# A branch hint at the head of every loop turn, on every engine

## The reference

```python
# 1: window attention with fake quantization (fq: int8 rounding by a scale from the tensor's largest value)
xw = windows of 7x7 pixels                       # 1024 windows, 49 tokens, 192 channels
q, k, v = split(fq(xw) @ fq(Wqkv).T + bqkv);  q, k, v = fq(q*SCALE), fq(k), fq(v)
attn = fq(einsum('bhmc,bhnc->bhmn', q, k)) + fq(bias)      # 12 heads of 16
attn = softmax(fq(attn));  out = fq(attn @ v) @ fq(Wout).T + bout
# 2: ConvNeXt block
y = depthwise_conv_7x7(x) + dw_b;  y = layernorm_channels(y) * ln_g + ln_b
y = gelu(y @ w1 + b1);  y = global_response_norm(y);  return x + y @ w2 + b2
```

## Time and profile before

| | us |
|---|---|
| three timed runs: median (lowest to highest) | 5646.66 (5645.17 to 5656.78) |
| the profiled execution | 5641.34 |
| its span, from the first to the last instruction | 5639.0 |
| qkv_range, qkv, range stages (rounded windows) | 270, 425, 650 |
| attention, project, conv, MLP loops (rounded windows) | 1275, 380, 460, 1090 |

### The profile page before, as it was taken

One profiled execution on the slowest core, in us unless ns is written; L12 is line 12 of the kernel. 1 busy time (PEld: TensorE's weight loads), 2 busy tenths in 40 slices (PEclk: granted clock), 3 DMA queues, 4 the chain that ended last, 5 costly groups with the idle time before them and its releaser, 6 DMA issues. The chain is left out here.

```text
span 5639.0 us, 117675 instructions
## 1 busy us (share of the span) xinstructions
PE 4267.6 (76%) x40394; PEld 2607.0 (46%) x40394; DVE 4318.8 (77%) x7490; ACT 3015.7 (53%) x5346; POOL 1539.3 (27%) x1649
## 2 busy tenths in 40 slices
PE   0787995555548777777774566699759999999999
PEld 0334553222226666666664444344334555555454
DVE  6898996999999888888886555000079999999986
ACT  0764672000008777777773556344355666666664
POOL 1103331000006555555554322000022222222220
PEclk9996555555559999999997777899969999999999
DMA  7864664333333332332332677788711222222222
GB/s 298 218 171 128 197 193 115 64 65 63 66 55 80 80 82 75 81 82 75 80 82 69 247 286 245 270 289 286 254 57 60 93 85 86 83 81 83 78 72 66
DMA packets 226218, 724.24 MB, mean 128 GB/s; under 512 B 34954, under 2 KB 132746, under 8 KB 205194
## 3 DMA queue, kind: packets, MB, share of 16 engines
q1 hardware_dynamic: 182346, 524.67, 32.4%
q0 software_dynamic: 43584, 195.21, 10.1%
HBM read 428.25 MB, written 291.50 MB: 128 GB/s over the span
## 5 line engine op out<-in xcount | busy, mean ns | idle before, releaser
L866 ACT ACTIVATE attn_int<-p_psum,scalars 128x588 int8<-128x588 f32 x512 | 384.8, 752 | 1045.6 <-PE p_psum L534 1020.9
L789 POOL TENSOR_TENSOR exp_lo<-exp,exp_hi 128x294 f16<-128x294 f32 x1024 | 779.6, 785 | 559.5 <-ACT exp_hi L860 556.6
L1551 PE MATMUL out_psum<-gelu_hi,w_parts 128*128 128x448 f16 x2016 | 605.3, 355 | 58.0 <-DVE w_parts L1727 30.9
L534 PE MATMUL range_psum<-q_diag,k_diag 128*128 128x196 bf16 x1536 | 364.8, 373 | 330.8 <-DVE p_min L652 328.7
L885 DVE SCALAR_TENSOR_TENSOR logit_int<-attn_int,scalars,bias_products 128x588 f16<-128x588 int8 x512 | 502.7, 982 | 124.7 <-ACT attn_int L866 96.4
L1623 DVE BATCH_NORM_STATS2 ln_stats<-z_img 128x6 f32<-128x192 f32 x448 | 125.9, 343 | 557.4 <-DMA z_img<-zd 556.9
L1587 ACT ACTIVATE gelu_pair<-h_psum,b_rows,w_unscale 128x448 f32<-128x448 f32 x448 | 324.8, 729 | 412.8 <-PE h_psum L1503 248.8
L831 PE MATMUL o_psum<-a_v,exp_hi 128*128 128x34 f16 x6144 | 383.1, 179 | 209.7 <-DVE a_o L909 191.5
L1287 PE MATMUL conv_psum<-c_in,toeplitz 128*128 128x448 f16 (+1 forms) x2304 | 469.7, 366 | 60.8 <-DMA dwb<-in_L_conv_dw_b_dram 60.6
L1503 PE MATMUL h_psum<-ln_parts_T,w_hi 128*128 128x448 f16 x2016 | 493.8, 354 | 18.8 <-DVE w_in L1686 16.9
L1551 PE MATMUL out_psum<-gelu_lo,w_parts 128*128 128x448 f16 x1344 | 475.7, 354 | 0.0
(11 more groups left out here) (313 smaller groups left out, 10008.2 us busy)
## 6 DMA issues: line engine op xcount, KB each, us to landing
k_diag<-kd SPq DMA_DIRECT2D x128, 384.0 KB, 5.1
toeplitz<-gd SPq DMA_DIRECT2D x48, 1024.0 KB, 16.5
yd<-y_out POOLq DMA_DIRECT2D x16, 2880.0 KB, 26.9
c_in<-yd SPq DMA_DIRECT2D x24, 1920.0 KB, 9.2
zd<-c_out POOLq DMA_DIRECT2D x24, 1792.0 KB, 13.7
z_img<-zd SPq DMA_DIRECT2D x16, 2688.0 KB, 9.2
x_chunk<-in_x_dram SPq DMA_DIRECT2D x12, 3136.0 KB, 9.9
x_img<-in_x_dram SPq DMA_DIRECT2D x16, 2352.0 KB, 16.0
```

What stands on the lines that cost most here:

```text
L534: last = nc.tensor.matmul(out[:, g, 0:HG * N], kt[:, g].rearrange("p o n -> p (o n)")[:, j::UP], q[:, g, :, j * N:(j + 1) * N], start=True ...
L789: last = nc.gpsimd.tensor_tensor(el[r][:, :, 2 * a, 0:N], src[:, :, a], eh[r][:, :, 2 * a, 0:N], ALU.subtract)
L866: nc.scalar.activation(a1[l % 2][:].rearrange("p (g n) -> p g n", g=G), pp[:, 0:G, 0:HG * N], ACT.Copy, scale=col(s, CP)).then_inc(a1d, 1)
L1551: last = nc.tensor.matmul(po[:, t, 0:TCH], w, hx[:, f, cols], start=f == 0 and x == 0, stop=f == NF - 1 and x == len(steps) - 1)
```

## The change

A new function `loop` opens a loop on one engine with a branch hint, and `peeled`, `images` and `turns` use it in place of `eng.Fori`. The first instruction of each turn, on each engine, then names the compare-and-branch at the end of the turn and says that it is likely taken. The rest of the program is as it was; the loop's bodies are one instruction longer, and all code behind a loop lies one instruction further on for each loop ahead of it on its engine. A loop that runs at most once would get no hint; there is none here.

```diff
+def loop(eng, first, end):
+
+    return eng.bass.Fori(first, end, engines=[eng.engine], hint_back_edge=True)
+
 def peeled(eng, n, body):
     body(0, True)
     if n > 1:
-        with eng.Fori(1, n) as i:
+        with loop(eng, 1, n) as i:
             body(i, False)
...
         def images(eng, image):
             image(0, True, lambda k: True)
-            with eng.Fori(1, IMG // 2 - 1) as i:
+            with loop(eng, 1, IMG // 2 - 1) as i:
                 image(i, False, lambda k: True)
...
         def turns(eng, turn):
             turn(0, True, True, True, True)
-            with eng.Fori(1, IMG - 3) as i:
+            with loop(eng, 1, IMG - 3) as i:
                 turn(i, False, True, True, True)
```

## The result

The changed kernel takes 5679.06 us (median; the runs lie between 5661.9 and 5717.9), the kernel before beside it 5645.91 us. The ratio is 1.0063, with an interval from 1.0048 to 1.0078. So the change makes the kernel slower, by about 0.6%, where I had forecast 5590 us. Its profiled execution has a span of 5677.7 us against 5639.0 us before, 38.7 us more.

A forecast was written before the change was run, and what follows sets the result against it. The prediction took TensorE's 14 attention back-edges, stalled on instruction fetch, as the bound. 5641.3 - 59 saved + 2 for hints = 5584 us, forecast as 5590 us since the timed median lies 5.3 us higher; range 5570 to 5655 us.

The forecast's parts named there:

- What bounds the kernel: Attention loop: TensorE's taken back-edge, median 5.29 us, 14 times, waits for instruction fetch and holds all engines.
- Taken away: TensorE's 14 attention back-edges go from 5.29 to 0.215 us, 5.08 us each, 71 us, all on the path.
- late next: Block behind TensorE's attention loop head: 127 instructions last 3.3 us, so up to 1.8 us of waiting returns each turn.
- the case that it works: Likeliest case, attention branch finds its target in place: 59 us saved, 5590 us (5571 to 5606), chance 0.45.
- A prefetcher that looks one block ahead has 6.6 us of warning: TensorE's attention branch: argument against the hint coming too late; 256 instructions at 26 ns give some 6.6 us.
- The head moves on by 3: TensorE's attention loop head shifts by three earlier loops' hints, leaving about 127 instructions in its block instead of 130.
- Comes too late: Rival: TensorE's attention hint gives only 0.2 us of warning or is ignored; 5641 to 5647 us, chance 0.32.
- Served second: Rival: at TensorE's attention branch the useless next block is fetched before the target; 62 us slower, 5709 us, chance 0.15.
- moves on a block: Rival: attention branch finds its target, but the block behind the head's waits; about 20 us saved, 5627 us, chance 0.08.
- The hints' own cost: One hint per turn and engine, 86 turns, about 0.05 us each: 4 us uncovered, taken as 2 us.
- Slower: Whole kernel slower than before: chance 0.15, from the target being fetched second at TensorE's attention branch, 5709 us.
- wrong altogether: Sign: another engine's small loop begins to fetch every turn, with q14 packets inside loops; no size given.

The follow-up runs named there:

- Slot 100: Kernel before with TensorE's attention loop head at instruction 100 of its fetch block: 5630.8 us without hint (0.9983), 5560.3 us with that loop's hint (0.9866).
- slot 157: Kernel before, no hints, TensorE's attention loop head put at instruction 157 of its fetch block, as in the changed kernel: 5656.9 us, 1.0041.
- slots 148: Kernel before with TensorE's attention loop head at instruction 148 of its fetch block: 5658.3 us without hint (1.0025), 5666.3 us with it (1.0035).
- slot 40: Kernel before plus TensorE's attention hint alone, loop head at instruction 40 of its fetch block, branch at instruction 175 of its own: 5575.9 us, 0.9886.
- slot 0: Kernel before plus TensorE's attention hint alone, loop head at the first instruction of a fetch block, branch at instruction 135: 5640.2 us, 0.9991.

## Why the prediction failed, step by step

**What bounds the kernel: right.** The 14 back-edges of TensorE in attention are on the path. Slot 100 shows it: with the branch at 0.45 us, VectorE's 5 us gap is gone and the time falls by 70.5 us.

**"Taken away": right in size, wrong in whether.** I had 71 us for all 14. Between slot 100 without and with the hint the branches shrink by 14 x 4.83 = 68 us, and the kernel by 70.5 us. A hinted branch costs 0.45 us, not the 0.215 us that I took. In the changed kernel the term is zero.

That 68 and 70.5 us nearly agree is partly luck, for two terms cancel. A mean turn is 5.20 us shorter in the traces. Of that, 4.83 us is the branch, and another 1.2 us is won from the branch to the first edge: without the hint TensorE's clock falls to the lower level at each of the 14 branches, with it the clock stays at the upper one at ten of them (58 us at the lower level over the loop instead of 143). The first edge then takes 1.3 us back. This last is what I had as "late next" (1.8 us). The clock was in my sum nowhere. With the head well placed the whole change saves 71 us, more than the 59 that I took for the case that it works.

**"A prefetcher that looks one block ahead has 6.6 us of warning": the step that failed.** From it I gave the likeliest case its 0.45, and the sum its -59 us; what came of that term is 0. The trace of before already spoke against it: 13 packets for 13 blocks, none behind the branch's own. The step from there to "nothing is fetched between the entry to the block and the branch, so nothing can be redirected" was written down as a rival and not believed. The hint worked with the branch 4.7 us behind the entry to its block (slot 175), failed in 12 of 14 turns at 3.0 us (slot 135), and here it had 0.4 us.

The Trainium skill (Runtime: NRT & Kernel Launch, section "Instruction fetch mechanics") says that prefetch is purely sequential. The traces of the kernel before and of the changed one agree with that. Slot 100 contradicts it: 12 packets instead of 13 a turn and a back-edge of 0.45 us say that a hint can turn one fetch away from the sequence. The measurement decides.

**"The head moves on by 3": wrong, and the source of the loss.** It moved by 31. I counted the instructions that TensorE itself gains and took that for the shift. The changed kernel then has 99 instructions behind its head instead of 127, and the next block is late by 1.0 to 1.9 us in every turn. I had expected that penalty (1.8 us) only as the price of a cured branch. It came behind uncured branches: 130 instructions had been enough cover for the next block, and 99 are not. My sum held no term for it, nor for VectorE's 4.9 us at the start of the stage, which probably has the same root.

**"Comes too late": the right rival with the wrong time.** Its mechanism is what happened, and TensorE's one hint alone gives its time (5649.1 us beside 5646.3 us; I had 5641 to 5647 us). For the whole change it lacked the term of the moved code: the place of TensorE's loop alone costs 0.41%, 0.22 to 0.60%, and hints on the other engines, which move the code nearly as far, 0.44%. The changed kernel's 0.63% (0.48 to 0.78%) lies at the upper end of both. VectorE's halt, which the place alone does not have, is 4.9 us or 0.09% of it. Whether anything is left beyond that can't be told within these intervals.

**"Served second" and "moves on a block": did not occur.** The branch never took 8 to 10 us as a rule (longest 6.4 us in the changed kernel), and by the packet counts the redirected fetch replaces the useless one instead of standing behind it. Two single branches look like the former, in kernels without a hint on this loop: 7.23 us (slot 157) and 7.69 us (hints on the other engines), each with two packets 0.3 and 0.5 us apart and 14 in the turn.

**The hints' own cost: within what I took.** Medians of 31 to 41 ns each (56 ns at most) against my 50 ns, and nothing measurable with all of them beside slot 100. What the runs show of their cost comes through where they push code.

**The chances.** Slower had 0.15, all of it from one mechanism that did not occur. My sign for "wrong altogether", packets of q14 inside the loops, did not show either (44 in the whole run, 43 before). What happened, a shift of code against fetch blocks on TensorE itself, stood in my text as a fixed number instead of as an unknown with two ends. A head anywhere in its block would have been the honest bound, and slots 100 to 157 without a hint span 0.9983 to 1.0041. The median came out 24 us above the top of the range.

## What to carry to other kernels

A branch hint pays only for a loop whose body does not stay on the engine, and only if the branch lies far enough behind the first instruction of its own fetch block: here it worked at 175 instructions or more and failed at 135 (12 of 14 turns) and at 36 or fewer. Put the loop's head so that both hold, the branch late in its block and plenty of code left behind the head, and leave the loops whose branches take 0.2 us alone. Any edit, even one to another engine's program, can move a large loop against its fetch blocks by enough to cost 0.4%, so before a small loss is explained by what an edit does, see whether the halts have moved. And price an idle stretch of TensorE with the clock behind it, not by its own length alone.

## What the runs showed of the hardware beyond that

- A branch hint takes a median of 31 ns on ScalarE, GpSimd and SyncE (41 ns on SyncE in the MLP), 39 ns on VectorE and 31 to 40 ns on TensorE.
- With its target in time, a hinted back-edge of the large loop takes 0.37 to 0.48 us at slot 100; those of TensorE's small loops take 0.21 us without a hint and 0.22 us with one.
- A taken branch to a block that is not there costs about the same whatever its place: medians of 5.2 to 5.5 us in all kernels where it is cold.
- Entering a placed loop costs one taken branch more, 0.19 us where its block has come (slots 148 and 157) and 5.2 to 5.5 us where not (slots 0 to 100); with every hint and slot 100 it was 0.56 us.
- The entry to the branch's block and the next packet lie 1.6 us apart at slot 100 and 3.0 us at slot 40; at slot 0 mostly no packet comes within the 3.0 us to the branch. What starts a fetch was not settled.
